# Input tiles asked for at the end of a slot, stores moved behind the skewed reads, and a last tile stored in three parts

## What is computed

```python
def layer(x, w, b):
    f = group_norm(x, groups=32)
    fn = f / max(norm(f, axis=channels), 1e-12)
    fp = pad(fn, 2 pixels on each side)
    # 25 similarities of a pixel with its 5 x 5 neighbours
    vol = [sum(fp[:, :, r:h + r, c:w + c] * fn, axis=channels) for c in range(5) for r in range(5)]
    return x + relu(einsum('oc,bchw->bohw', w, concat([f, vol])) + b)
out = layer(layer(x, w0, b0), w1, b1)
```

## Time and profile before

| | |
|---|---|
| time, median of 3 runs | 490.61 us (490.59 to 491.08) |
| the profiled execution: its own time | 490.72 us |
| its span, first to last instruction | 489.0 us |
| busy: PE, DVE, ACT, POOL | 436.7, 367.2, 291.6, 111.2 us |
| mean granted TensorE clock | 0.986 of full speed |
| transfers | 65.88 MB, mean 135 GB/s |

### The profile page before, as it was taken

The page is one execution under the profiler, slowest core; times in us unless marked ns, Lnnn a source line. Parts: engine busy times, 40 slices in busy tenths (PEclk is TensorE's granted clock), DMA queues, the critical chain, the costliest instruction groups (busy, mean ns, idle before and its releaser), DMA issues.

```text
span 489.0 us, 13950 instructions
## 1 busy us (share of the span) xinstructions
PE 436.7 (89%) x5896; PEld 222.6 (46%) x5896; DVE 367.2 (75%) x871; ACT 291.6 (60%) x349; POOL 111.2 (23%) x168
## 2 busy tenths in 40 slices
PE   0368599677989999999998999999999999999996
PEld 0334245332445445454544455554545454544442
DVE  6899788768969798879878797979888787424322
ACT  1754474839388575949385767767584939513231
POOL 4421401031311404031312304040403131223100
PEclk9989899989999999999999999999999999999999
DMA  7662543132320555368666764040313143545322
GB/s 293 271 192 72 150 159 88 47 75 61 91 64 23 152 173 168 101 222 251 205 190 232 220 230 129 24 124 29 101 40 96 50 149 90 172 155 179 120 118 86
DMA packets 33989, 65.88 MB, mean 135 GB/s; under 512 B 11756, under 2 KB 21028, under 8 KB 33926
## 3 DMA queue, kind: packets, MB, share of 16 engines
q1 hardware_dynamic: 24014, 55.95, 34.7%
q0 software_dynamic: 9792, 8.92, 7.5%
q10 hardware_dynamic: 120, 0.11, 0.1%
HBM read 33.54 MB, written 28.87 MB: 128 GB/s over the span
## 4 chain that ended last, share of the span: by engine, by line
PE 57%; DVE 21%; ACT 7%; DMA 6%; issue 5%; POOL 2%; SPq 1%; ACTq 0%; DVEq 0%
PE conv_ps L611 45%; DVE stats L866 6%; PE conv_ps L620 4%; DVE operands L914 4%; PE gram_ps L533 4%; ACT v L731 3%; DMA vol<-corr_h 2%; DVE xs L999 2%; ACT operands L723 2%; PE gram_ps L546 2%; DMA rn_far<-rows_dram 1%; DVE operands L920 1%; DMA skew<-band_dram 1%; DVE wl L987 1%; ACT act_out L760 1%
## 5 line engine op out<-in xcount | busy, mean ns | idle before, releaser
L611 PE MATMUL conv_ps<-operands,wh 128*128 128x512 f16 x1024 | 329.1, 384 | 6.6 <-ACT act_out L760 4.3
L611 PE MATMUL conv_ps<-operands,wl 128*128 128x512 f16 x512 | 196.0, 383 | 0.0
L611 PEld LDWEIGHTS conv_ps<-operands,wh 128*128 128x128 f16 x1024 | 101.6, 99 | 127.6 <-ACT act_out L760 6.5
L760 ACT ACTIVATE act_out<-conv_ps,bias,wdown 128x512 f32<-128x512 f32 x128 | 95.4, 772 | 88.3 <-PE conv_ps L620 85.9
L999 DVE TENSOR_TENSOR xs<-xs,act_out 128x512 f32<-128x512 f32 x128 | 85.9, 685 | 37.7 <-ACT act_out L760 37.7
L723 ACT ACTIVATE operands<-xs,affine 128x1024 f16<-128x1024 f32 x64 | 93.1, 1462 | 17.5 <-DVE affine L906 17.5
L914 DVE TENSOR_TENSOR operands<-v,operands 128x1024 f16<-128x1024 f32 x64 | 79.3, 1240 | 27.2 <-ACT v L731 23.1
L866 DVE BATCH_NORM_STATS2 stats<-xs 128x6 f32<-128x512 f32 x128 | 79.9, 684 | 2.4 <-DMA xs<-in_x_dram 2.4
L611 PEld LDWEIGHTS conv_ps<-operands,wl 128*128 128x128 f16 x512 | 50.5, 99 | 56.1 <-issue 2.4
L731 ACT ACTIVATE v<-xs,affine 128x1024 f32<-128x1024 f32 x55 | 72.6, 1319 | 0.4 <-DVE operands L914 0.4
L533 PE MATMUL gram_ps<-operands 128*32 128x108 f16 (+1 forms) x2048 | 49.2, 215 | 15.0 <-DVE operands L920 9.8
(11 more groups left out here) (75 smaller groups left out, 221.0 us busy)
## 6 DMA issues: line engine op xcount, KB each, us to landing
xs<-in_x_dram SPq DMA_DIRECT2D x32, 512.0 KB, 7.4
out_dram<-xs SPq DMA_DIRECT2D x32, 512.0 KB, 3.0
band_dram<-band SPq DMA_DIRECT2D x64, 120.0 KB, 2.3
skew<-band_dram SPq DMA_DIRECT2D x32, 222.5 KB, 3.0
vol<-corr_h POOLq DMA_DIRECT2D x48, 50.0 KB, 3.1
rows_dram<-rows SPq DMA_DIRECT2D x32, 65.8 KB
rows_dram<-rows SPq DMA_DIRECT2D x32, 63.3 KB
mirror<-rows_dram POOLq DMA_DIRECT2D x14, 110.9 KB, 2.5
```

Of the source, the lines that this page charges most:

```text
L611: pe.matmul(conv_ps[:, g % 4, :], w[:, l, t, m * P:(m + 1) * P], opnd[:, u % RING, part, t, n * HALF:(n + 1) * HALF], start=(t == 0 and w ...
L760: act.activation(in_rows(act_out[:, g % AOUT, :]), by_rows(conv_ps[:, g % 4, :]), ACT.Relu, bias=bias[:, l, m:m + 1], scale=wdown[:, l, m: ...
```

## The change

Three things change. In SP's list the stores of tiles 0 and 1 go behind the write and the skewed read of the band; the loads of a new image go from the middle of the slot to its end, behind the rows, and are issued one slot earlier in the count (for unit k - 2 in place of k - 3). For the last group of the last unit (u = 15, g = 7) the 512 pixels are worked in two parts of 256: 13 matmuls, one eviction and one addition for each part, each in a bank and a buffer of its own. The last tile is stored as 512, 256 and 256 pixels, each as soon as its part is added.

```diff
+        LAST_PARTS = 2
+        QUARTER = HALF // LAST_PARTS
+        PIECES = ((slice(0, HALF), 1), (slice(HALF, HALF + QUARTER), 2), (slice(HALF + QUARTER, PIX), 3))
+        def parts(u, g):
+            n = LAST_PARTS if u == UNITS - 1 and g == GROUPS - 1 else 1
+            return [slice(i * HALF // n, (i + 1) * HALF // n) for i in range(n)]
...
                     for t in tiles:
+                        if u == UNITS - 1 and t == KT - 1:
+                            for part, done in PIECES:
+                                sp.wait_ge(x_sum, GROUPS * u + 2 * t + done)
+                                sp.dma_start(out_v[b, :, t, part], xs[:, ring_slot(b), t, part]
+                                             ).then_inc(x_out[t], 16)
+                            continue
...
             for k in range(STEADY, SLOTS):
-                tiles_out(k - 2, (0, 1))
                 if valid(k):
                     band_through_dram(k)
-                tiles_in(k - 3)
+                tiles_out(k - 2, (0, 1))
...
                 tiles_out(k - 2, (2, 3))
                 if valid(k):
                     rows_to_dram(k)
+                tiles_in(k - 2)
             for t in range(KT):
-                sp.wait_ge(x_out[t], 16 * BATCHES)
+                sp.wait_ge(x_out[t], 16 * (BATCHES + (len(PIECES) - 1 if t == KT - 1 else 0)))
...
                 wait(pe, relu, GROUPS * u + g - 3)
+                if len(parts(u, g)) > 1:
+                    return
+                channel_products(u, g, slice(0, HALF), g % 4)
...
-                pe.matmul(conv_ps[:, g % 4, :], wvol[0:96, l, m * P:(m + 1) * P],
-                          vol[0:96, u % 2, n * HALF:(n + 1) * HALF], start=False, stop=True).then_inc(conv, 1)
+                pieces = parts(u, g)
+                for i, cols in enumerate(pieces):
+                    bank = (g + i) % 4
+                    if len(pieces) > 1:
+                        wait(pe, relu, GROUPS * u + g + i - 3)
+                        channel_products(u, g, cols, bank)
+                    pe.matmul(conv_ps[:, bank, cols], wvol[0:96, l, m * P:(m + 1) * P],
+                              vol[0:96, u % 2, n * HALF + cols.start:n * HALF + cols.stop],
+                              start=False, stop=True).then_inc(conv, 1)
```

More of the change, by code:

```diff
@@ L608, in channels, with channel_products @@
                 wait(pe, relu, GROUPS * u + g - 3)
+                if len(parts(u, g)) > 1:
+                    return
+                channel_products(u, g, slice(0, HALF), g % 4)
+            def channel_products(u, g, cols, bank):
+                l, m, n = unit_layer(u), g // 2, g % 2
                 for t in range(KT):
                     for w, part in ((wh, 0), (wl, 0), (wh, 1)):
-                        pe.matmul(conv_ps[:, g % 4, :], w[:, l, t, m * P:(m + 1) * P],
-                                  opnd[:, u % RING, part, t, n * HALF:(n + 1) * HALF],
+                        pe.matmul(conv_ps[:, bank, cols], w[:, l, t, m * P:(m + 1) * P],
+                                  opnd[:, u % RING, part, t, n * HALF + cols.start:n * HALF + cols.stop],
                                   start=(t == 0 and w is wh and part == 0), stop=False)
@@ L757, in rectified @@
                 l, m = unit_layer(u), g // 2
[L758 to L761, removed]
+                for i, cols in enumerate(parts(u, g)):
+                    act.wait_ge(conv, GROUPS * u + g + i + 1)
+                    wait(act, x_sum, GROUPS * u + g + i - AOUT + 1)
+                    act.activation(in_rows(act_out[:, (g + i) % AOUT, cols]), by_rows(conv_ps[:, (g + i) % 4, cols]),
+                                   ACT.Relu, bias=bias[:, l, m:m + 1], scale=wdown[:, l, m:m + 1]).then_inc(relu, 1)
             deviations(0)
@@ L996, in added @@
                 m, n = g // 2, g % 2
-                xt = xs[:, ring_slot(unit_batch(u)), m, n * HALF:(n + 1) * HALF]
-                dve.wait_ge(relu, GROUPS * u + g + 1)
-                dve.tensor_tensor(xt, xt, act_out[:, g % AOUT, :], ALU.add).then_inc(x_sum, 1)
+                for i, cols in enumerate(parts(u, g)):
+                    xt = xs[:, ring_slot(unit_batch(u)), m, n * HALF + cols.start:n * HALF + cols.stop]
+                    dve.wait_ge(relu, GROUPS * u + g + i + 1)
+                    dve.tensor_tensor(xt, xt, act_out[:, (g + i) % AOUT, cols], ALU.add).then_inc(x_sum, 1)
             dve.memset(gram_ps[:, :, :], 0.0).then_inc(gram_clear, 1)
```

## The result

The changed kernel takes 496.51 us (median of 4 runs, 496.15 to 497.13) against 490.80 for the kernel before: 1.0124 times as long, interval [1.0087, 1.0161]. It is 1.2% slower, where 487.4 was forecast, and lies outside the range. The profiled execution takes 496.79 us, span 495.0, mean granted clock 0.978.

A forecast was written before the change was run, and what follows sets the result against it. TensorE was taken as the bound, with losses in slots 8 and 15 and the tail: 490.72 - 1.92 - 0.43 - 1.15 + 0.3 = 487.5 profiled, 487.4 as median of the runs. Range 486.6 to 489.9.

The forecast's parts named there:

- The bound: TensorE, busy end to end in plain slots; where it bounds, a microsecond off its waits is one off the time.
- Slot 8's collision: In slot 8 `vol` transfers meet the new image's loads and TensorE waits; moving the loads saves 1.92 us.
- the collision is not resolved: Rival, slot 8: `vol` is as late beside the stores, the 1.92 us stays, 489.3 us; chance 0.08.
- small matmuls: Rival, last group: weight loads bound the 256-column matmuls, 2.6 us more, 490.0 us; chance 0.05.
- Part 1: Loads moved to the end of the slot: saves 1.92 us in slot 8, costs 0.3 over slots 7 to 9.
- the last view lands near 220.7: Slot 7, moved loads ahead of the views: last view 0.8 us later than today, within cover.
- 1.33 of cover: Between VectorE finishing neighbour values (227.81) and TensorE's transposes (229.14): lateness up to 1.33 us costs nothing.
- views at the full price: Rival, slots 7 to 9: last view takes 7.2 us, transposes 1.8 us late each, 492.5 us; chance 0.10.
- Part 2: Stores behind the skewed read: gains 0.43 us in slot 15; band behind loads in slots 7 to 9 costs 0.
- band behind the loads: Rival, slots 7 to 9: band lands after the loads, 1.0 us over cover a slot, up to 490.1; chance 0.17.
- The 0.43 us of slot 15: TensorE's idle time before slot 15's transposes, neighbour values late behind a 4.83 us skewed read; forecast to go.
- Part 3: Tail, last group in two parts: eviction saves 0.28, addition 0.27, final store 0.6; sum 1.15 us.

The follow-up runs named there:

- y5: Kernel before plus extra 2 MB reads of image 3 behind the rows of slots 10 to 12, after the next unit's local products: 505.96 us, ratio 1.0319.
- y3: Kernel before plus extra reads of image 3 behind the rows of slots 10 to 12: 498.88 us, ratio 1.0187.
- z: Changed kernel with the loads back in the middle of the slot, same as x3, with more runs: 488.33 us, ratio 0.9969.
- x3: Changed kernel with only the loads put back to the middle of the slot, behind the stores of tiles 0 and 1: 488.12 us, ratio 0.9982.
- x2: Kernel before with the last tile in three parts alone, loads and stores in the old order: 489.46 us, ratio 0.9994.
- y6: Kernel before plus extra reads of image 3 behind the skewed read of slots 11 to 13: 491.31 us, ratio 0.9997.
- y1: Changed kernel with half of each image's loads (tiles 2 and 3) moved back behind the mid-slot stores: 488.99 us, ratio 0.9979.
- x4: Changed kernel with the loads of images 5 to 7 cut to 16 of 1024 pixels a tile: 486.96 us, ratio 0.9955.

## Why the prediction was wrong

**The bound** was right: in these slots a microsecond of TensorE's waiting is one of time.

**Slot 8's collision** went, as forecast. `vol` landed in 3.9 to 5.4 us over the three slots for "about 5", and the wait for it (1.6 us) is gone. The rivals "the collision is not resolved" and "small matmuls" are out: the 26 small matmuls start 0.109 us apart.

**The failed step** is the cost of Part 1: "the last view lands near 220.7", 1.4 us before the loads end, priced at 0.3. The loads' end was forecast well (222.1; measured 222.93, in a slot that began 0.5 us later). But the last view landed 1.4, 1.9 and 1.1 us *after* that end. The 1.4 "before" had been taken from `vol` in the earlier trace rows, whose transfers were issued half a microsecond behind the first load and so shared the engines with all of them; the views are issued 2.5 to 6 us behind it. I had read that as an advantage ("a good part is through"), but the last view, issued last, also came last. From there the prediction's own arithmetic holds: 4.0 us late less 1.33 of cover is 2.67, and slot 7 became 2.76 longer. The rival "views at the full price", with 0.10, came nearest. Its 7.2 us were close to what the last view took (8.1, 6.9 and 6.1), and its 5.4 us of waits came as 2.54 + 2.42, in two slots. Its 492.5 fell short by 4 us mainly because of two things that no term held: the `issue` wait of 1.96 us, and the lower clock in slot 8 (1.3 us, and 0.4 in the transposes).

**A second step failed beside it**, in Part 2: the band was to land "about a microsecond later than today", under the same cover, and was put down as 0. Its last write landed at 224.50 (220.66 before), 3.8 us later and 1.6 behind the loads, and the skewed read landed at 228.83 (224.83 before): counted from the start of the slot 3.5 us later, for 1.33 of cover. So the rival "band behind the loads" was right about the band, too; its price is mostly hidden under that of the views.

That "views at the full price" got 0.10 rests on a weighing that the bounds did not support: the rows that showed POOL's transfers beside loads were at 6.5 to 7.8 us and at 8.95, so the 7.2 that was taken as the worst was only their middle, and the step from there to "lands near 220.7" was an interpolation. The sentence that the prediction cites from the Trainium skill, "DMA: Bandwidth & Descriptors", section "Queues, rings and completion order", has each engine alternate between rings. The trace agrees that the two queues share: three to six of the seven views landed before the last load did. What I concluded from it, that POOL's views do not wait, did not hold: the `rn_far` views took 5.2 to 8.1 us (2.9 to 5.3 before), and the last one landed behind the last load in all three slots. The same section has a second rule, which I did not weigh: a transfer's completion is signalled by a write that lands only after every earlier write of that DMA engine, across its queues. By it a view could be reported late behind loads that stand in another queue. In the trace this is the small part: the last data packet of the views ended at 223.29, 252.72 and 280.96, 0.8 to 1.1 us before they counted as landed (0.6 in slot 7 of the kernel before). So the data themselves came late, and signalling adds at most 0.5 us to their lateness.

**Slot 9** lost nothing before its transposes: slot 8's time at the lower clock came behind the transposes and put slot 9's views ahead (the last one landed 7.87 us into the slot, 10.16 in slot 7), and the `issue` wait, which came first, gave them another 1.96 us. That wait is nearly all of the 2.1 us that the slot lost. About this wait the Trainium skill, "Runtime: NRT & Kernel Launch", section "Instruction fetch mechanics", says that each engine's sequencer fetches its instructions in blocks over a DMA queue of its own, and that this is "mostly hidden". The first half agrees with q8 in the trace (packets of 16 KB, and the 16 waits that end behind one) and with y5; the second does not hold here beside a 2 MB burst: 1.96 us in the changed kernel, 7.1 in y3.

**Part 2**, as far as the stores go, costs nothing and gains 0.6 to 1.0 us in single executions (z and x3 against x2). The 0.43 us of slot 15 was no term of it.

**Part 3** was 1.15 and is 1.28: eviction 0.78 to 0.56 (forecast 0.50), addition 0.69 to 0.43 (0.42), store 2.6 to 1.8 (2.0). The last small matmul starts 0.14 later (0.11) and streams 0.11 less (0.11), so 0.03 are lost there (0).

## What to carry to other kernels

A burst of loads has no price of its own; the work that is issued behind it pays, so look at each place in the cycle for what comes next there and how much cover that has (here 2 MB in each of three slots cost nothing behind the skewed read in y6 and 8.2 us behind the rows in y3; in slot 8 of the kernel before, where the views were late already, the place behind the skewed read cost the 1.6 us of waiting for `vol`). A transfer issued behind a burst is best priced as landing after the burst, until a row shows otherwise. Keep a burst away from a block of many short matmuls: 14 of the 16 waits without a releaser stood in the local products, and y5, which held the loads back until these were done, had none. Whether longer matmuls would have helped was not tried.

## What the runs showed of the hardware that was not expected

- Instructions can be late: TensorE stood still inside its local products for 1.96 us (the changed kernel) and 1.4 to 2.8 us at a time (y3) while loads held the DMA engines, and not at all when the loads waited for those products (y5). It went on 1.25 to 1.64 us after a packet on q8 had ended, in 16 of 16 cases.
- Small transfers of another queue share the DMA engines with a burst and still come late: 5.2 to 8.1 us for 27.7 KB beside 2 MB (the changed kernel), 2.6 to 3.6 beside 1 MB (y1), 2.5 to 3.9 beside almost nothing (x4).
- The granted clock fell to 0.50 behind one wait of 2.42 us and did not behind one of 2.54. What tells the two apart stays open.
- A store of 128 KB lands in 1.8 us, where one of 512 KB takes 2.6.
- The head, the same in all these kernels, ended anywhere from 160.8 to 164.8 us in the profiled executions, while the rest of the one kernel that was profiled twice agreed within 0.4. So a change of 0.3% shows in the rest sooner than in the times.
